# Splitting 24 of 33 pairs, with the low parts shared between VectorE and GpSimd, three up banks and one down bank

## The reference, cut to what matters

```python
h  = concat(fine_embed[ids], softmax(W.T[ids] + b) @ coarse_embed)       # "early": embedding
x  = layernorm(h); xn = rmsnorm(x)
x  = x + mem_scale * (((xn q)(xn k)^T * decay) v) o^T                      # "late": linear attention
h  = h + x + op_scale * gelu(rmsnorm(x) @ read @ mix + bias) @ write.T     #   and operator
x3 = layernorm(h)
p, i = top_k(softmax(x3 @ router.T + bias), 6); p = p / (p.sum() + 1e-9)   # gates, with a capacity cut
h  = h + mean_over_2_shared(down(silu(x3 gate) * (x3 up))) \
       + sum_over_64_experts(gate_e * down_e(silu(x3 gate_e) * (x3 up_e)))
```

## Time and profile before

| | us |
|---|---|
| median of 3 runs | 718.22 |
| lowest, highest | 716.77, 1065.27 |
| span of the profiled execution, first to last instruction | 716.0 |
| TensorE busy | 692.8 (97%) |
| VectorE busy | 523.4 (73%) |
| GpSimd busy | 466.5 (65%) |
| ScalarE busy | 350.6 (49%) |

### The profile page before, as it was taken

One profiled execution on the slowest core, in us unless ns is written; L12 is line 12 of the kernel. 1 busy time (PEld: TensorE's weight loads), 2 busy tenths in 40 slices (PEclk: granted clock), 3 DMA queues, 4 the chain that ended last, 5 costly groups with the idle time before them and its releaser, 6 DMA issues.

```text
span 716.0 us, 9975 instructions
## 1 busy us (share of the span) xinstructions
PE 692.8 (97%) x3133; PEld 524.7 (73%) x3133; DVE 523.4 (73%) x1074; ACT 350.6 (49%) x609; POOL 466.5 (65%) x345
## 2 busy tenths in 40 slices
PE   7788899999999999999999999999999999999998
PEld 7666677777777777777777777777777777777775
DVE  5677686987768867887769877788678766674444
ACT  3543455446454374445553474544745435534432
POOL 5035477776677767685676776676775656676664
PEclk9999999999999999999999999999999999999999
DMA  5504232243323333333333433333333433334431
GB/s 204 226 1 128 71 118 104 85 133 105 111 106 114 114 108 99 120 113 102 118 103 101 128 103 103 118 110 109 114 105 102 125 103 105 115 112 124 138 123 60
DMA packets 48869, 80.17 MB, mean 112 GB/s; under 512 B 9520, under 2 KB 13744, under 8 KB 48816
## 3 DMA queue, kind: packets, MB, share of 16 engines
q1 hardware_dynamic: 47792, 77.44, 33.4%
q0 software_dynamic: 1024, 2.10, 1.2%
HBM read 76.35 MB, written 3.15 MB: 111 GB/s over the span
## 4 chain that ended last, share of the span: by engine, by line
PE 88%; DVE 4%; issue 3%; POOL 2%; ACT 1%; DVEq 0%; POOLq 0%
PE bank_y L467 16%; PE bank_g L481 8%; PE bank_g L482 8%; PE bank_g L483 8%; PE bank_u L483 8%; PE bank_u L481 8%; PE bank_u L482 8%; PE bank_y L464 4%; PE bank_y L462 4%; PE bank_y L461 4%; POOL hid L1040 1%; PE bank_f L408 1%; PE bank_f L386 1%; PE bank_f L402 1%; PE bank_f L445 1%
## 5 line engine op out<-in xcount | busy, mean ns | idle before, releaser
L1040 POOL TENSOR_TENSOR hid<-hid,gate_rows 128x512 f32<-128x512 f32 x256 | 374.2, 1470 | 195.4 <-DVE hid L881 193.0
L623 ACT ACTIVATE hid<-bank_g 128x512 f32<-128x512 f32 x264 | 156.6, 599 | 264.4 <-PE bank_g L483 261.8
L881 DVE TENSOR_TENSOR hid<-hid,bank_u 128x512 f32<-128x512 f32 x264 | 178.7, 681 | 128.3 <-PE bank_u L483 78.2
L481 PE MATMUL bank_g<-x_hi,gate_hi 128*128 128x512 f32 x264 | 142.9, 541 | 0.0
L467 PE MATMUL bank_y<-hid,w_down 128*128 128x512 f32 x272 | 138.7, 591 | 0.0
L887 DVE TENSOR_TENSOR hid_lo<-hid,hid_hi 128x512 fp32r<-128x512 f32 x128 | 110.2, 861 | 2.4 <-ACT hid_hi L629 2.4
L482 PE MATMUL bank_g<-x_hi,gate_lo 128*128 128x512 f32 x264 | 104.5, 396 | 0.0
L483 PE MATMUL bank_g<-x_lo,gate_hi 128*128 128x512 f32 x264 | 104.5, 396 | 0.0
L481 PE MATMUL bank_u<-x_hi,up_hi 128*128 128x512 f32 x264 | 103.9, 393 | 0.1
L483 PE MATMUL bank_u<-x_lo,up_hi 128*128 128x512 f32 x264 | 103.8, 393 | 0.0
L482 PE MATMUL bank_u<-x_hi,up_lo 128*128 128x512 f32 x264 | 103.8, 393 | 0.0
(11 more groups left out here) (209 smaller groups left out, 857.1 us busy)
## 6 DMA issues: line engine op xcount, KB each, us to landing
gate_rows<-gates_dram SPq DMA_DIRECT2D x512, 128.0 KB, 2.9
w_down<-down_t_dram SPq DMA_DIRECT2D x3, 704.0 KB, 14.5
out_dram<-later SPq DMA_DIRECT2D x7, 256.0 KB, 3.1
hid<-gate_t_dram SPq DMA_DIRECT2D x2, 704.0 KB, 5.8
gates_dram<-gates_t SPq DMA_DIRECT2D x8, 128.0 KB, 2.2
gate_rows<-up_t_dram SPq DMA_DIRECT2D x1, 704.0 KB, 5.7
later<-up_t_dram SPq DMA_DIRECT2D x1, 704.0 KB, 9.9
raw<-gate_t_dram SPq DMA_DIRECT2D x1, 704.0 KB, 11.0
```

Source lines behind the costliest of these rows:

```text
L481: pe.matmul(o, w_hi[name][:, p, :], x3_hi[par][:, :], start=True, stop=False)
L623: act.activation(hid[:, slot(par, p), :], bank_g[(p + par) % 2][:, :], ACT.Silu).then_inc(sem("silu"), 1)
L881: dve.tensor_tensor(hid[:, s, :], hid[:, s, :], bank_u[(p + par) % 2][:, :], ALU.mult)\
L1040: pool.tensor_tensor(hid[:, s, :], hid[:, s, :], gate_rows[:, row, :], ALU.mult)\
```

## The change

The diff does the following.

- Split pairs are now all with p % 4 in 1, 2, 3: 24 of 33. hid_hi and hid_lo get a third buffer (SPLIT_RING).
- The low parts of pairs with p % 4 == 2 (2, 6, ..., 30, eight) are made by GpSimd (`pool_lo`), in its iteration p+2 behind that iteration's gate multiply; VectorE keeps the sixteen odd ones. TensorE waits for the one or the other before the third down matmul.
- bank_u has three banks, bank_y one. So pair 0's down product of a batch waits until the last batch's sum has been copied out, and that copy moves from iteration 5 to 4.
- AHEAD is 4: one more pair of batch 0 goes through gate and up in the prologue, three of them ahead of the gates' transposes and the warming transposes there.
- x1 moves to ScalarE (iteration 5, Identity with a bias and a scale per token); xn2 too, except in batch 0. For x1's bias GpSimd makes shift1 from the mean and inv1 in two small operations behind inv1.
- var1 (two small operations) and var3 (one) move from VectorE to GpSimd, in front of inv1 and inv3.
- Some buffers share memory (vals with xn2_t, decay_full with x1), and ones_row becomes one broadcast column.

```diff
-SPLIT_LAG, SPLIT_RING = 2, 2
-SPLITS = PAIRS // 2
+SPLIT_LAG, SPLIT_RING = 2, 3
+SPLIT_PAIRS = tuple(p for p in range(PAIRS) if p % 4)
+SPLITS = len(SPLIT_PAIRS)
+POOL_LO = tuple(p for p in SPLIT_PAIRS if p % 4 == 2)
+DVE_LO = tuple(p for p in SPLIT_PAIRS if p not in POOL_LO)
...
-ACT_AT = dict(xn_hi=2, y_hi=4, z=6, ffn_t=5, ...
+ACT_AT = dict(xn_hi=2, y_hi=4, x1=5, z=6, ffn_t=4, squares=9, squares2=10, cluster_exp=10, xn2=11, ...
...
-AHEAD = 3
+AHEAD = 4
...
-        bank_u = [bank(f"bank_u{i}") for i in range(2)]
-        bank_y = [bank(f"bank_y{i}") for i in range(2)]
+        bank_u = [bank(f"bank_u{i}") for i in range(3)]
+        bank_y = bank("bank_y")
...
         def down(pe, b, par, p):
-            y = bank_y[par][:, :]
+            y = bank_y[:, :]
+            if p == 0:
+                wait(pe, "ffn_t", b)
...
-                pe.wait_ge(sem("hid_lo"), split_count(b, p))
+                if p in POOL_LO:
+                    pe.wait_ge(sem("hid_lo_pool"), len(POOL_LO) * b + POOL_LO.index(p) + 1)
+                else:
+                    pe.wait_ge(sem("hid_lo"), len(DVE_LO) * b + DVE_LO.index(p) + 1)
                 pe.matmul(y, down_hi[:, j, :], hid_lo[:, k, :], start=False, stop=False).then_inc(sem("down_done"), 1)
...
+            if p == ACT_AT["x1"]:
+                act.wait_ge(sem("shift1"), b + 1)
+                wait(act, "x2", b)
+                for t in range(TILES):
+                    last = act.activation(x1[:, t, :], emb[par][:, t, :], ACT.Identity,
+                                          bias=shift1[:, t:t + 1], scale=inv1[:, 0, t:t + 1])
+                last.then_inc(sem("x1"), 1)
+            if p == ACT_AT["xn2"] and b:
+                act.wait_ge(sem("inv2"), b + 1)
+                for t in range(TILES):
+                    last = act.activation(xn2[:, t, :], x2[:, t, :], ACT.Copy, scale=inv2[:, t:t + 1])
+                last.then_inc(sem("xn2"), 1)
...
             if p == POOL_AT["inv3"]:
+                pool.wait_ge(sem("mv3"), b + 1)
+                pool.tensor_scalar(var3[:, :], mv3[:, :, 1], LN_EPS, None, ALU.add).then_inc(sem("var3"), 1)
                 pool.wait_ge(sem("var3"), b + 1)
                 pool.tensor_tensor(inv3[:, :], var3[:, :], neg_half[:, 0:TILES], ALU.pow).then_inc(sem("inv3"), 1)
 
         def pool_early(pool, b, p):
             if p == POOL_AT["inv1"]:
+                pool.wait_ge(sem("mv1"), b + 1)
+                pool.tensor_scalar(var1[:, 0, :], mv1[:, :, 1], LN_EPS, None, ALU.add)
+                pool.tensor_scalar(var1[:, 1, :], mv1[:, :, 1], 1.0 + RMS_EPS, RMS_EPS * LN_EPS, ALU.mult, ALU.add)\
+                    .then_inc(sem("var1"), 1)
+                wait(pool, "x1", b)
                 pool.wait_ge(sem("var1"), b + 1)
                 pool.tensor_tensor(inv1[:, :, :], var1[:, :, :], neg_half[:, :].rearrange("p (k t) -> p k t", k=2),
                                    ALU.pow).then_inc(sem("inv1"), 1)
+                pool.wait_ge(sem("inv1"), b + 1)
+                pool.tensor_tensor(shift1[:, :], mv1[:, :, 0], inv1[:, 0, :], ALU.mult).then_inc(sem("shifts"), 1)
+                pool.wait_ge(sem("shifts"), b + 1)
+                pool.tensor_scalar(shift1[:, :], shift1[:, :], -1.0, None, ALU.mult).then_inc(sem("shift1"), 1)
...
+                if p - SPLIT_LAG in POOL_LO:
+                    pool_lo(pool, b, par, p - SPLIT_LAG)
+
+        def pool_lo(pool, b, par, p):
+            k = split_slot(b, p)
+            pool.wait_ge(sem("hid_hi"), split_count(b, p))
+            pool.tensor_tensor(hid_lo[:, k, :], hid[:, slot(par, p), :], hid_hi[:, k, :].bitcast(F32), ALU.subtract)\
+                .then_inc(sem("hid_lo_pool"), 1)
```

More of the change, by code:

```diff
@@ L46 @@
 LAG = 4
-SPLIT_LAG, SPLIT_RING = 2, 2
-SPLITS = PAIRS // 2
+SPLIT_LAG, SPLIT_RING = 2, 3
[3 more added lines that the diff above has]
+DVE_LO = tuple(p for p in SPLIT_PAIRS if p not in POOL_LO)
 DOWN_HI_AT, DOWN_LO_AT = 10, 14
 GATHER_AT = (1, 2, 3, 4)
-DVE_AT = dict(xn=0, xn_lo=2, x1=5, xn_dec=5, y_lo=4, scores=6, state=6, x2=8, result=10, logits=9, xn2=11, exp_sum=12,
+DVE_AT = dict(xn=0, xn_lo=2, xn_dec=5, y_lo=4, scores=6, state=6, x2=8, result=10, logits=9, xn2=11, exp_sum=12,
               h=15, bn1=16, h2=17, bn3=17, mv1=18, x3=19, x3_lo=21, router=24, prob=26, top=27, chosen=28, gates=29,
@@ L59 @@
              router=23, gates_t=30)
-ACT_AT = dict(xn_hi=2, y_hi=4, z=6, ffn_t=5, squares=9, squares2=10, cluster_exp=10, exp_t=12, xn2_t=13, vals=14,
+ACT_AT = dict(xn_hi=2, y_hi=4, x1=5, z=6, ffn_t=4, squares=9, squares2=10, cluster_exp=10, xn2=11, exp_t=12, xn2_t=13, vals=14,
               x3_hi=21, router_exp=24)
@@ L475, in gate_up @@
                     pe.wait_ge(sem(f"split_lo{CHUNK_OF[n, p]}"), 1)
[L476 to L480, removed]
+            if b == 0 and p == 2:
+                pe.wait_ge(sem("h"), 2)
+            for name, out_bank, freed, count in (("gate", bank_g[q % 2], "silu", q - 1),
+                                                 ("up", bank_u[q % 3], "up_used", q - 2)):
+                wait(pe, freed, count)
+                o = out_bank[:, :]
                 pe.matmul(o, w_hi[name][:, p, :], x3_hi[par][:, :], start=True, stop=False)
@@ L699, in dve_late @@
                 last.then_inc(sem("xn"), 1)
-            if p == DVE_AT["x1"]:
-                for t in range(TILES):
-                    last = dve.tensor_scalar(x1[:, t, :], emb[par][:, t, :], mv1[:, t, 0:1], inv1[:, 0, t:t + 1],
-                                             ALU.subtract, ALU.mult)
-                last.then_inc(sem("x1"), 1)
             if p == DVE_AT["xn_dec"]:
@@ L742, in dve_late @@
                    .then_inc(sem("x2"), 1)
-            if p == DVE_AT["xn2"]:
+            if p == DVE_AT["xn2"] and b == 0:
                 dve.wait_ge(sem("inv2"), b + 1)
@@ L905, in dve_sequence @@
                     split_lo(dve, PAIRS + p)
+                if first and p == 0:
+                    dve_up(dve, b, par, AHEAD - 2)
                 if p >= AHEAD - 1 or not first:
                     dve_up(dve, b, par, p)
-                if p >= SPLIT_LAG and is_split(p - SPLIT_LAG):
+                if p - SPLIT_LAG in DVE_LO:
                     dve_lo(dve, b, par, p - SPLIT_LAG)
-                elif not first and p < SPLIT_LAG and is_split(p - SPLIT_LAG + PAIRS):
+                elif not first and p - SPLIT_LAG + PAIRS in DVE_LO:
                     dve_lo(dve, b - 1, 1 - par, p - SPLIT_LAG + PAIRS)
```

71 lines of the change are left out of this document (38 added, 33 removed).

## The result

The changed kernel takes 782.37 us (median of 4 runs, 780.46 to 782.98) against 717.87 for the one before: a ratio of 1.090, interval 1.088 to 1.092. It is slower, as forecast, but by 65 us and not by 22. The forecast time (740) and its range (711 to 755) are both missed. One of the four runs of the kernel before, of 1065.27 us, is left out of the ratio.

The account below looks back on a forecast made before the run. TensorE was taken to bound the steady batches. Terms -10.9 + 19.0 + 9.1 + 3.0 + 1.3 + 0.7 = +22.2 us on the 716.0 span gave 738.2, a median of 740.4, range 711 to 755.

Parts of the forecast that it names:

- The split's gain: Eight more split pairs a batch save TensorE 0.17 us each, 64 of them, -10.9 us.
- The waits at pairs 18 and 22: TensorE waits for GpSimd's low parts: 3.1 us in six batches, 0.4 in the seventh (19.0); 1.3 in seven (9.1).
- The end of the run: Pair 30's low part stands behind GpSimd's last multiply and TensorE needs it to finish: +1.3 us.
- pair 2: Pair 30's earlier low part runs ahead of VectorE's xn: 0 to 1.2 us, 0.6 taken, five batches, 3.0.
- rival 3: Waits cool TensorE, mainly at pair 18: six batches add 6 to 12 us, 746 to 752; chance 0.18.
- VectorE and GpSimd also hold each other up: A low part on VectorE took 2.17 us while GpSimd worked without pause; two-SBUF-input VectorE operations and GpSimd's exclude each other.
- Pair 10 at 0: With xn2 off VectorE the chain comes about a microsecond earlier: no wait, at most 0.8 us in six batches.
- The prologue at +0.7: Prologue and first sequence: down_hi +0.9, third gate_up +1.2, x1 before z copy +0.4, less 1.8: +0.7 us.
- The -1.8: First sequence: x1 off VectorE gives back 1.8 of TensorE's 2.24 us wait before the state product.
- The third pair: Prologue: a third gate_up ahead of the gates' transposes puts them at 56.45 instead of 55.27 us, +1.2.
- x1 ahead of the z copy in the prologue: x1 on ScalarE stands before the z copy: +0.4 us, between 0 and 1.2.
- Small operations only weighed at pair 18: Five small GpSimd operations ahead of pair 20's multiply add 1.35 us to pair 18's wait.

Follow-up runs that it names:

- e15: e14 with GpSimd's gathers moved to iterations 14, 17, 26 and 31 of the sequence before: 714.53 us, ratio 0.996 to the kernel before the change.
- e3: The changed kernel with GpSimd's inv1 and its four small operations moved from iteration 20 to 25: 781.0 us.
- e7: The changed kernel with GpSimd's inv1 and its four small operations moved from iteration 20 to 24: 757.7 us.
- e2: The changed kernel with 24 transposes filling TensorE's wait between pair 18's second and third product in six sequences: 770.0 us.
- e5: e1 with GpSimd's four gathers moved from iterations 1 to 4 to iterations 27 to 30 of the sequence before: 728.8 us.
- e13: The changed kernel with pairs 2 and 26 whole, all low parts on VectorE, inv1 at iteration 24, first batch's x1 on VectorE: 722.09 us, ratio 1.006.
- e14: e13 with the third pair's gate and up products behind the gates' transposes in the prologue: 719.74 us, ratio 1.003.
- e6: e4 with GpSimd's inv1 and its four small operations moved from iteration 20 to 24: 719.6 us.
- e11: e6 with x1 of the first batch alone back on VectorE: 715.7 us.
- e4: The changed kernel with the eight pairs of GpSimd's low parts left whole, so 16 split pairs: 728.0 us.
- e1: The changed kernel with all 24 low parts on VectorE, none on GpSimd: 745.8 us.

## Why the prediction was wrong

**Right.** TensorE bound the steady batches. The split's gain: 0.17 us (e15). The waits at pairs 18 and 22: 3.1 and 1.3 forecast, 3.09 and 1.33 measured, released by GpSimd's low part. inv1 and its small operations belonged to pair 18's wait: 2.4 of the 3.09 us go with them (e3, e7). The end of the run: 1.3 forecast, 1.9. Pair 0's wait for the one down bank and the third up bank: nothing, as forecast. Forecast for pair 2: 0.6, measured up to 0.16. x1 on ScalarE needed no change of tables, as taken, but 1.64 us for its four operations and not 1.2 (24.59 us).

**Wrong, by its steps.**

1. *The clock was left out of the sum and priced too low as rival 3.* The rival had 1 to 2 us a batch, from half to all of what one short gap had cost in the first sequence. Behind pair 18's wait it was 2.7: 5.8 us between iterations 22 and 24, of which 3.09 are the wait. e2 shows it by itself, 10.9 us in all although part came up elsewhere. The Trainium skill's warning (TensorE: Matmul & The Clock Gate, HAM oscillation) agrees with the trace: the low clock came behind this wait in each of the five steady batches.
2. *"VectorE and GpSimd also hold each other up"* was written down without a term in the sum, but for pair 2's 0.6. I took the 2.17 us of the earlier trace rows as a given and did not ask which VectorE operation would fall into a longer run of GpSimd. It was the low part ahead of the scores: 4.73 us, and 1.75 us of TensorE a batch; e5 and e15 remove it by the gathers' place alone. The rows agree with the exclusive lock of which the Trainium skill speaks (SBUF — State Buffer, SBUF: two separate sides). What made it dear is that VectorE got in only behind GpSimd's run: the low part was at its start at 356.31 us, and GpSimd's operations of 356.73, 357.98 and 359.23 all went first.
3. *Pair 10 at 0, "at most 0.8".* In the steady batches 0.3 to 0.6. In the first sequence TensorE stood 2.64 us before it with a stretch at 1.2 GHz behind, 5.4 in all: I had carried the steady batch over to a sequence that has other work in it. Its hx was 1.4 us longer, beside VectorE's low part of the up weights; that this is the cause of the whole wait was not tested.
4. *The prologue at +0.7.* It was 4.5 by the ninth pair. The -1.8 that x1 on ScalarE was to give back came: the state product of the first sequence no longer waits, and the difference falls by 4.0 there, the clock included. What the sum lacked lies ahead of it: a first gate product 3.6 us late, and the y product's 2.59 us for the low part of x with a stretch at 1.2 GHz behind it, a wait that every run kept. The third pair, 1.2 forecast, is 2.4 (e13 against e14). x1 ahead of the z copy in the prologue, 0.4 forecast, is 3.9 in the single runs e6 and e11. Both figures hold what the clock did in that stretch, and its share is not settled.
5. *Small operations only weighed at pair 18.* e4 and e6 show a second way, by ScalarE's high part into the Silu, worth 1.3 us a batch (84.4 against 83.1); in the changed kernel this wait is not there, TensorE being late anyway.

Items 1 to 3 make up nearly all of the difference in a steady batch (2.7 + 1.75 + 0.8 of 5.7), items 3 and 4 most of the 13 us by which the first sequence and prologue missed theirs.

## What to carry to other kernels

A wait of some microseconds on TensorE has to be priced with the clock behind it, from a stretch of the same trace that has one. For work put on GpSimd, ask which VectorE operations will fall into the run of work that it makes longer, and look for a place where GpSimd only waits; one step moved to such a place (inv1 to iteration 24) was worth 23 us, to the next iteration nothing. A wait that is taken away can bring the low clock up at another (e2, e7). A first sequence needs its own sum.

## What the runs showed of the hardware

A VectorE subtraction of 128x512 with both inputs in SBUF took 0.68 us alone and up to 4.73 beside three GpSimd operations in a row, while the up product, one of its inputs in PSUM, kept 0.67 to 0.69 beside the same work. TensorE's fall to 1.2 GHz behind a 2.0 us wait was not a fixed thing: behind the state product it came in each of the five steady batches of e3 and e7, in three of five in e1 and e2, and in none of the changed kernel.
